# VectorE rotates q and takes the fourth softmax step ahead of the sum with the residual; a new order on GpSimd in the end phase, seven fixed tiles, tile counts from a table

## What is computed

```python
x = x + conv(ln_c(x))            # dilated, shifted 8x8 windows, 8 heads of 8 channels
#   q, k, v = x @ W_qkv + b; q, k rotated (rope)
#   softmax(q k^T * scale + mask) v; then @ W_proj + b_proj
t = t + ffn(ln_t(t))             # mixture of experts: 8 experts, top 2, hidden 682
#   probs = softmax(flat @ router_w.T); topk_probs, topk_idx = top_k(probs, 2); renormalised
#   h = silu(flat @ w1[e].T) * (flat @ w3[e].T); out += gate * (h @ w2[e].T)
```

## Time and profile before

| | |
|---|---|
| runs | 696.06, 697.98, 703.49 us, median 697.98 |
| profiled execution | 693.54 us |
| its span, first to last instruction | 691.2 us |
| so around the span | 2.3 us |
| busy share of the span | PE 86%, DVE 70%, ACT 60%, POOL 64% |
| mean granted clock of PE | 0.95 |
| PE: L473 of the first expert tile | 328.7 us |
| PE: L518 of the fourth and of the 51st tile | 364.8, 674.1 us |
| VectorE: counts, L1076 to L1126 | 335.08 to 338.07 us |

### The profile page before, as it was taken

How to read it: one execution, slowest core, us unless ns; L and a number is a source line. 1 busy time by engine, 2 the same in 40 slices (tenths; PEclk the granted TensorE clock), 3 DMA queues, 4 the chain that set the end, 5 groups by cost and what they waited for, 6 DMA issues and landing times.

```text
span 691.2 us, 20144 instructions
## 1 busy us (share of the span) xinstructions
PE 593.7 (86%) x5359; PEld 368.5 (53%) x5359; DVE 484.2 (70%) x1692; ACT 414.2 (60%) x934; POOL 440.0 (64%) x398
## 2 busy tenths in 40 slices
PE   1888888888888888852889999999999999999991
PEld 0466566656665556542445555555555555555550
DVE  2578878888878767763556667777676777776772
ACT  1678777778767767641345556555565565565560
POOL 1111777767767766546557876775766868666776
PEclk9999999999999999965599999999999999999996
DMA  9900000100000000001143444444434434344342
GB/s 328 295 10 9 26 27 25 33 25 25 25 24 25 24 23 24 26 25 37 45 85 39 53 43 44 50 41 48 50 38 50 44 43 52 38 50 48 38 52 16
DMA packets 85590, 34.67 MB, mean 50 GB/s; under 512 B 81966, under 2 KB 82478, under 8 KB 85038
## 3 DMA queue, kind: packets, MB, share of 16 engines
q0 software_dynamic: 26640, 9.90, 15.0%
q1 hardware_dynamic: 58910, 24.30, 14.3%
HBM read 20.21 MB, written 13.76 MB: 49 GB/s over the span
## 4 chain that ended last, share of the span: by engine, by line
PE 51%; issue 7%; DMA 5%; POOL 5%; DVE 4%; POOLq 1%; ACT 1%; DVEq 0%; ACTq 0%
PE bank L504 21%; PE bank L518 13%; POOL expert_rows L1225 3%; PE bank L473 3%; DMA expert_rows<-rows,slot_u 3%; PE bank L451 2%; PE bank L509 2%; PE bank L441 2%; PE bank L463 2%; PE bank L634 2%; DMA out<-y_early,meta 1%; PE bank L528 1%; DMA out<-y_out,token 1%; DVE smax L960 1%; PE bank L435 1%
## 5 line engine op out<-in xcount | busy, mean ns | idle before, releaser
L1313 POOL DMA_INDIRECT out<-y_out,token x144 | 222.8, 1547 | 89.2 <-DVE y_out L1136 53.1
L1225 POOL DMA_INDIRECT expert_rows<-rows,slot_u x144 | 147.8, 1027 | 79.2 <-issue 27.5
L504 PE MATMUL bank<-xs,w_sb 64*128 64x384 f32 x510 | 182.2, 500 | 4.7 <-DVE hid L1175 1.8
L505 PE MATMUL bank<-xs,w_sb 64*128 64x384 f32 x510 | 182.5, 501 | 0.0
L779 ACT ACTIVATE gate_h<-bank 128x384 f32<-128x384 f32 x255 | 125.2, 492 | 61.2 <-PE bank L505 43.6
L1175 DVE TENSOR_TENSOR hid<-gate_h,bank 128x384 f32<-128x384 f32 x255 | 140.4, 554 | 30.2 <-ACT gate_h L779 13.2
L504 PEld LDWEIGHTS bank<-xs,w_sb 64*128 64x128 f32 x510 | 92.0, 189 | 88.2 <-issue 39.4
L518 PE MATMUL bank<-hid,w_sb 128*64 128x384 f32 x612 | 110.5, 496 | 2.7 <-DVE hid L1175 2.7
L505 PEld LDWEIGHTS bank<-xs,w_sb 64*128 64x128 f32 x510 | 92.0, 189 | 0.0
L789 ACT ACTIVATE y_odd<-bank 64x384 f32<-64x384 f32 x51 | 24.9, 487 | 85.9 <-PE bank L518 82.0
L1168 DVE TENSOR_TENSOR y_t<-y_odd,bank 64x384 f32<-64x384 f32 x51 | 27.8, 546 | 56.3 <-ACT y_odd L789 53.4
(11 more groups left out here) (136 smaller groups left out, 977.2 us busy)
## 6 DMA issues: line engine op xcount, KB each, us to landing
xin<-expert_rows SPq DMA_DIRECT2D x51, 99.0 KB
xin<-expert_rows SPq DMA_DIRECT2D x51, 96.0 KB
w_sb<-w SPq DMA_DIRECT2D x1, 3072.0 KB, 22.1
out<-res_all SPq DMA_DIRECT2D x18, 128.0 KB
expert_rows<-rows,slot_u POOLq DMA_INDIRECT x144
out<-y_out,token POOLq DMA_INDIRECT x144
x_all<-x_win SPq DMA_DIRECT2D x1, 1664.0 KB, 8.6
res_all<-x_res SPq DMA_DIRECT2D x1, 1664.0 KB, 12.1
```

The costliest lines, as they stand in the source:

```text
L504: pe.matmul(ps_h[c % RING], w13_sb[0:C, e, c, :], xs[0:C, :], start=True, stop=True)
L505: pe.matmul(ps_g[c % RING], w13_sb[C:2 * C, e, c, :], xs[C:2 * C, :], start=True, stop=True).then_inc(s_h, 1)
L1225: pool.indirect_dma_start(rows_dram, bass.IndirectOffsetOnAxis(ap=slot_u[:, spar, i // 2, i % 2:i % 2 + 1], axis=0), rows[:, spar, i // 2, ...
L1313: pool.indirect_dma_start(out, bass.IndirectOffsetOnAxis(ap=token[:, c:c + 1], axis=0), y_out[:, c, :], None, compute_op=ALU.add).then_inc ...
```

## The change

It moves two things on VectorE, gives POOL another order in the end phase, makes four tiles of expert 0 fixed instead of three, and computes the numbers of tiles by comparison with a table.

```diff
-EARLY = (1, 1, 1, 0, 0, 0)
-OWN = 3
+EARLY = (1, 1, 1, 0, 0, 0, 0)
+OWN = 4
...
-K_COLS = 422
+K_COLS = 414 + E * MOST
...
                 if ok(b):
                     rotate(b, ps_k, k_st, 1, rope_k, s_kst, s_sum, b - G)
+                if ok(b):
+                    rotate(b, ps_q, q_st, 0, rope_q, s_qst, s_score, b - G)
                 if ok(new):
                     ln1_squares(new)
+                if ok(att_g):
+                    soften(att_g + 3, 3)
                 if ok(out_g):
                     after(dve, s_proj, out_g, -(G - 1))
...
                 if ok(out_g):
                     ln2_total(out_g)
-                if ok(b):
-                    rotate(b, ps_q, q_st, 0, rope_q, s_qst, s_score, b - G)
                 if ok(out_g):
                     ln2_average(out_g)
                 if ok(route):
                     pick(route)
-                if ok(att_g):
-                    soften(att_g + 3, 3)
...
-            dve.tensor_copy(cnt_f[:], ps_cnt).then_inc(s_tstep, 1)
+            dve.tensor_tensor(padrow_f[:], ps_cnt, late_base[:], ALU.add).then_inc(s_tstep, 1)
             dve.wait_ge(s_tstep, 1)
...
+            dve.tensor_tensor(over[:], padrow_f[:].unsqueeze(2).to_broadcast([P, E, MOST]), tile_ends, ALU.is_gt).then_inc(s_tstep, 1)
+            dve.tensor_copy(padrow_i[:], padrow_f[:])
             dve.wait_ge(s_tstep, 2)
...
+            dve.reduce_sum(til_m[:], over[:], AX).then_inc(s_tstep, 1)
             dve.wait_ge(s_tstep, 3)
...
                     hold(pool)
-                    scatter(to, (0, 1, 2, 3), par)
-                    pause(send, par, 4)
-                    scatter(to, (4, 5), par)
-                    if ok(out_g):
+                    scatter(to, (0, 1), par)
+                    if b == TILES:
                         root(ln2_rstd, ln2_vare, s2vare, s2rstd, s2xn, out_g)
-                    scatter(to, (6, 7), par)
-                    pause(send, par, 8)
+                    scatter(to, range(2, 2 * G), par)
+                    if b == TILES:
+                        root(ln2_rstd, ln2_vare, s2vare, s2rstd, s2xn, out_g + G)
+                    else:
+                        pause(send, par, 2 * G)
```

More of the change, by code:

```diff
@@ L71 @@
 BIG = -1.0e30
-THIRD, THIRD_SHIFT = 171, 9
-assert SUB == 3 and all(x * THIRD >> THIRD_SHIFT == x // SUB for x in range(TOKENS // P + SUB + 1))
+MOST = TOKENS // SLOTS
+assert MOST * SLOTS == TOKENS
 MASKED_PER_IMAGE = PER_IMAGE // 3
@@ L90 @@
 FIRST_TILES = 5 * G
-K_IDENT, K_ROPE, K_SUM, K_HEAD, K_VMASK, K_IOTA, K_BASE, K_SKIP, K_TIL = 0, 128, 256, 384, 388, 390, 398, 406, 414
-K_COLS = 422
+K_IDENT, K_ROPE, K_SUM, K_HEAD, K_VMASK, K_IOTA, K_BASE, K_SKIP, K_ENDS = 0, 128, 256, 384, 388, 390, 398, 406, 414
+K_COLS = 414 + E * MOST
 W_QK, W_V, W_BIAS, W_VBIAS = 0, 128, 192, 194
@@ L132, in build @@
         early_rows = consts[:, K_SKIP:K_SKIP + E]
-        tile_base = consts[:, K_TIL:K_TIL + E]
+        tile_ends = consts[:, K_ENDS:K_ENDS + E * MOST].rearrange("p (e t) -> p e t", e=E)
         ident_b = constb[:, B_IDENT:B_IDENT + P]
@@ L189, in build @@
         late_base = sb("late_base", [P, E])
[L191 to L195, removed]
+        over = sb("over", [P, E, MOST])
         til_m = sb("til_m", [P, E])
@@ L1075, in _ @@
             dve.wait_ge(s_cnt, 1)
-            dve.tensor_copy(cnt_f[:], ps_cnt).then_inc(s_tstep, 1)
+            dve.tensor_tensor(padrow_f[:], ps_cnt, late_base[:], ALU.add).then_inc(s_tstep, 1)
             dve.wait_ge(s_tstep, 1)
-            dve.tensor_tensor(padrow_f[:], cnt_f[:], late_base[:], ALU.add).then_inc(s_tstep, 1)
+            dve.tensor_tensor(over[:], padrow_f[:].unsqueeze(2).to_broadcast([P, E, MOST]), tile_ends, ALU.is_gt).then_inc(s_tstep, 1)
+            dve.tensor_copy(padrow_i[:], padrow_f[:])
@@ L1079, in _ @@
             dve.wait_ge(s_tstep, 2)
-            dve.tensor_tensor(til_f[:], padrow_f[:], tile_base, ALU.subtract).then_inc(s_tstep, 1)
+            dve.reduce_sum(til_m[:], over[:], AX).then_inc(s_tstep, 1)
             dve.wait_ge(s_tstep, 3)
-            dve.tensor_copy(til_i[:], til_f[:]).then_inc(s_tstep, 1)
-            dve.tensor_copy(padrow_i[:], padrow_f[:]).then_inc(s_tstep, 1)
+            dve.tensor_tensor_scan(ends_f[:], til_m[:], zero8[:], float(len(EARLY)), ALU.add, ALU.add).then_inc(s_tstep, 1)
@@ L1084, in _ @@
+            dve.wait_ge(s_tstep, 4)
+            dve.tensor_scalar(ends_mf[:], ends_f[:], float(-BEHIND), None, ALU.add).then_inc(s_tstep, 1)
             dve.wait_ge(s_tstep, 5)
[L1085 to L1104, removed]
             dve.tensor_copy(ends_m[:], ends_mf[:])
@@ L1390, in constants @@
     kf[:, K_SKIP:K_SKIP + E] = SKIP
-    kf[:, K_TIL:K_TIL + E] = np.arange(E) * REGION + np.array(SKIP) - (SLOTS - 1)
+    ends = (np.arange(E) * REGION + np.array(SKIP))[:, None] + np.arange(MOST)[None, :] * SLOTS
+    ends[:, 0] = -1
+    kf[:, K_ENDS:K_ENDS + E * MOST] = ends.reshape(-1)
     kb = np.zeros((P, B_COLS), np.float32)
```

## The result

On the chip of the first comparison the changed kernel took 723.34 us (719.62 to 724.72, 4 runs) against 697.02 (693.83 to 703.49): ratio 1.037, interval 1.033 to 1.041. The prediction was 680. On two other chips the same two kernels gave 0.979 (0.974 to 0.984) and 0.977 (0.973 to 0.981), which is the prediction's 680 / 698 = 0.974 but for 0.3 to 0.5 per cent.

A forecast was written before the change was run, and what follows sets the result against it. VectorE, working or waiting before L1042, was taken to bound stage 1's unmasked bodies. Gains 8.8 + 1.2 + 3.7 + 3.9 - 0.2 = 17.4 us took 693.54 to 676.1; the median lies 4.4 higher: 680, range 671 to 690.

The forecast's parts named there:

- Scatters 4 and 5: POOL, stage 1: may start after the earlier softmax step, at most 1.3 us earlier; no cost was put on it.
- the slower one: Rival, chance 0.04: PE stands some 5 us at the longer shared-add wait, its clock falls in the tiles: 705.
- POOL's slack: Stage 1: POOL's waits of 1.6 us in a 15.84 us period counted as spare, leaving 14.3 as its own length.
- unmasked bodies: Stage 1: VectorE's idle before L1042 filled, eight periods of 14.4 us instead of 15.5, a gain of 8.8 us.
- the masked ones: Stage 1: PE's path lies closer; six masked bodies and the first drain body gain 3.7 us, 0.53 each.
- the bodies ahead: Stage 1: two bodies ahead of the unmasked eight, same hole but fewer instructions, gain 0.6 each, 1.2 us.
- before `rden`: Stage 1, sign of being wrong: VectorE's freed time comes back as a wait there of over 1 us.
- End phase: Drain and expert tiles: new POOL order, faster counts and a fourth fixed tile gain 3.9 us.
- the first shared add: POOL, end phase: starts at 379.9 instead of 378.30, but for the fifth tile, so 4.9 us earlier in the tiles.
- some 5 us: End phase: VectorE's wait for the first shared add grows to this from 2.52 us.
- The tile stream: End phase, PE: first tile 8.1 us earlier by early root and counts; one tile is some 6.5 us.
- PE's clock is below 1: Sign of being wrong, behind the first tiles; 1 us was taken off for half clock after PE stands.

The follow-up runs named there:

- soften_alone: Kernel before with only the fourth softmax step moved ahead of L1042 on VectorE: 729.67, ratio 1.044.
- after_third: The changed kernel, unaltered, run again on another chip (fifth set) against the kernel before: 668.55, ratio 0.977.
- before_again: The kernel before, unaltered, run again for its trace on a chip with prompt signals (fourth set): 683.46, one run.
- the split: POOL's scatter 5 moved behind the ln2 root: alone on the kernel before 684.98, ratio 1.001; on the changed kernel 668.91, ratio 0.977.
- end_alone: The changed kernel with VectorE's stage 1 order put back, so only end phase, fixed tiles and counts are new: 695.81, ratio 0.994 against the kernel before.
- both moves: Kernel before with rotation of q and fourth softmax step moved ahead of L1042, nothing else: 721.66, ratio 1.033.

## Why the prediction was right or wrong

**What failed** is one sentence: "Scatters 4 and 5 may start after the earlier softmax step, at most 1.3 us earlier." It was priced at nothing. The scatters started 0.6 and 1.0 us earlier, joined scatter 3 to a train, and on the chip of the comparison that cost 27.2 us by the last rotation of k (308.04 against 280.87). No rival had this mechanism; the slower one was put in the wrong place. The nearest ground in it was the rule that it cites from the Trainium skill, "SBUF — State Buffer", "Who interferes with whom", on a VectorE instruction that blocks GpSimd. It was priced at 3 us less gain and is not what happened: the long scatter is there (1.23 at 109.34), but PE pays.

**What I could have read.** The trace of before already had it. The release of the 1.05 us wait in the earlier trace rows was read as POOL's slack ("15.84 - 1.6 = 14.3"), not as a gap that something lived on. And 66 of 281 of PE's signals were late there, the value projection's by 0.6 us in every unmasked body. The grouped lines show "issue" for half of L1042's idle time (7.6 of 15.1), and no view shows that a signal of PE comes late: for that one needs the semaphore events beside the ends of the matmuls. The Trainium skill, "Perfetto Trace Analysis", "Summary: the profiler window per engine type", says that TensorE's window ends at an estimated end and leaves the way of its semaphore out. The trace agrees that the row doesn't hold the signal's way: it ends at 109.80, and the signal lands at 113.76.

**Half clock** is a consequence that adds to it: the granted clock in the unmasked bodies was 0.85 instead of 1.00, in stretches that follow the torn matmuls. soften_alone has bodies with the train at both clocks (its value projection's signal lands at 9.5 us in each):

```profile
125.72:142.63 16.91, 14.04 (x177) 9.84 (x177) 13.17 (x51) 11.72 (x30) 11.23 (x14) 1.00 0.09 24
142.63:159.81 17.18, 14.11 (x178) 9.89 (x177) 13.18 (x51) 12.02 (x30) 11.24 (x14) 1.00 0.08 23
159.81:179.27 19.46, 16.52 (x172) 11.15 (x173) 13.36 (x51) 11.81 (x29) 12.19 (x15) 0.78 0.08 21
```

Beside the 15.2 and 15.8 of the kernel before, waiting alone adds 1.3 to 1.7 us a body there, and the half clock another 2.3 to 2.6. For the changed kernel itself the 19.4 us can't be divided, since none of its unmasked bodies with a train ran at full clock.

**Stage 1 by its own steps**, where signals are prompt (after_third and before_again, on two chips; unmasked, then masked bodies):

```profile
54.89:170.69 115.80, 103.74 (x1422) 76.48 (x1421) 105.27 (x401) 95.15 (x234) 81.69 (x104) 0.99 0.10 26
170.69:260.63 89.94, 81.78 (x1080) 57.64 (x1079) 78.93 (x298) 71.16 (x174) 66.53 (x83) 0.98 0.10 28
```

```profile
55.32:179.29 123.97, 105.47 (x1422) 75.31 (x1421) 104.38 (x400) 95.42 (x234) 83.58 (x104) 1.00 0.09 25
179.29:272.38 93.09, 81.84 (x1081) 56.62 (x1080) 78.08 (x298) 72.06 (x174) 68.22 (x83) 1.00 0.10 27
```

The unmasked bodies give 8.2 us (8.8 forecast; periods of 13.9 to 14.6 and one of 15.6, against the 14.4 taken), the masked ones 3.1 and the bodies ahead 0.4 (3.7 with the first drain body, and 1.2). The 0.2 us for the larger constants rest on no row; the first rotation of k comes at 16.79 us instead of 16.70. VectorE's idle time before L1042 is 0.0 instead of 15.1 us; 1.8 us in eight bodies came back before `rden`, less than the 1 us each that would have proved me wrong. There the mechanism and its size were right; the term for the bodies ahead was three times too large.

**End phase.** On the same two traces the last root came 8.2 us earlier than stage 1 alone explains (314.17 to 294.20, less 11.8; forecast 6.7), the last scatter 2.8 (344.39 to 329.89; forecast 3.4, though 318.8 and 23 steps of 1.26 and two pauses make 351.2 and not 351.7), the first shared add 2.6 us later than that alone (368.75 to 359.62; forecast 1.6). So VectorE's wait for it grew as the prediction said, but to more than twice its "some 5 us":

```profile
362.77 0.22 DVE L1139 COPY token<-meta 128x2 uint16<-128x2 uint16 x1 [11.84 <-DMA out<-y_out,token]
```

From the last rotation of k to the last L518 the kernel before takes 392.2 us and the changed one 390.6: 1.6 us won there, 3.9 forecast. The tile stream was mis-sized: the fourth tile's L518 comes 23.7 us earlier (353.87 to 330.14), the add only 9.1, and the fixed tile gives back 6.5 of the difference; the wait grows by the rest, from 3.9 us in the kernel before. But a longer wait alone costs nothing, since the add sets the time. The missing 2.3 us have two other causes. The shared add came 1.0 us later than forecast. And PE stood 9.7 us during the wait, and then its granted clock fell:

```profile
362.77:380.00 17.23, 16.79 (x92) 9.73 (x94) 11.04 (x35) 7.96 (x17) 12.64 (x9) 0.83 0.39 39
```

```profile
363.21 0.98 PE L500 MATMUL bank<-xs,w_sb 64*128 64x384 f32 x1 [9.68 <-DVE y_out L1141]
```

From the end of the wait to the last L518 the changed kernel takes 288.4 us, and the kernel before 292.5 with one tile of 6.5 us more: 2.4 us lost, where the prediction took off 1. So its own sign "if PE's clock is below 1 behind the first tiles" came true here. In before_again the same stretch, after a wait of 3.9, has 1.00. With the split the end phase takes 388.1 to 388.7 us (four traces), 3.5 to 4.0 less than the kernel before. Where signals are held the tiles come later; end_alone won 4.5, which its trace doesn't show.

**The sum** of stage 1 and the end phase there is 0.4 + 8.2 + 3.1 + 1.6 = 13.3 us, 681.5 to 668.2 in spans, where 17.4 was forecast.

## What to carry to other kernels

An engine that waits "for nothing" ahead of its DMAs may be keeping them apart: if a change moves the releaser of such a wait, price the new train of DMAs, on every engine that signals beside it. Compare the time at which a matmul ends with the time at which its semaphore lands before the idle time of a reader is called a round trip. Where one computation can stand between two indirect DMAs, try it there: the split cost nothing where signals are prompt (1.001), and with both moves it gave 0.982 where they are not, against 1.033 without it (on two chips of that kind). And let a verdict of 3% rest on more than one chip.

## What the runs showed of the hardware

On three sets of runs PE's completion signals landed up to 4 us late in stage 1 and 6.6 in the end phase while POOL issued indirect DMAs, and PE itself then passed one to a few matmuls every 0.75 us; VectorE's and ACT's signals were not held. Where a root of 1.04 us stood in place of the third scatter, the signal landed 0.5 us after the second scatter's end. On three other chips there was none of it with the same code and the same issue times, and the kernel before was 1.7 to 2.3% faster there (685 against 697 to 701). The cause in the chip stays open.
